# A recommender tower on one core: 24 steps in one table, another order of loads, and other shares for VectorE and GpSimd

## What is computed

```python
e = jnp.stack([tbl_0[ids[:, 0]], ..., tbl_31[ids[:, 31]]], axis=1)     # (512, 32, 16)
x0 = xk = e
for W in (W0, W1, W2):                                                # (32, hk, 64)
    xk = relu(einsum('bmd,bhd,mhk->bkd', x0, xk, W))
    outs.append(sum(xk, axis=2))
h = concatenate([concatenate(outs, axis=1), dense_ctx], axis=1)       # 192 + 16 columns
y = relu(relu(h @ W_top1 + b_top1) @ W_top2 + b_top2) @ W_top3
```

## Time and profile before

| | us |
|---|---|
| Median of 3 runs (380.64 to 382.44) | 381.08 |
| Span of the profiled execution, first to last instruction | 395.6 |
| TensorE matmuls busy | 292.4 (74%) |
| VectorE busy | 278.7 (70%) |
| GpSimd busy | 276.8 (70%) |
| ScalarE busy | 60.3 (15%) |
| Mean granted TensorE clock, 1.0 is full | 0.931 |
| Read from HBM | 60.17 MB |

### The profile page before, as it was taken

How to read it: one execution, slowest core, us unless ns; L and a number is a source line. 1 busy time by engine, 2 the same in 40 slices (tenths; PEclk the granted TensorE clock), 3 DMA queues, 4 the chain that set the end, 5 groups by cost and what they waited for, 6 DMA issues and landing times.

```text
span 395.6 us, 3778 instructions
## 1 busy us (share of the span) xinstructions
PE 292.4 (74%) x1252; PEld 94.2 (24%) x1252; DVE 278.7 (70%) x145; ACT 60.3 (15%) x72; POOL 276.8 (70%) x204
## 2 busy tenths in 40 slices
PE   0001400578979969998889599699849999999995
PEld 0000100222223313322223123132212333333341
DVE  0002200779978986999789779599799999999600
ACT  1001000221210312112120131121021022211021
POOL 5777772289999888999998885999980807856000
PEclk9999955699999996999999989699985999999999
DMA  7229589988522999978449899764289994340000
GB/s 220 43 52 300 161 292 337 335 262 252 170 63 85 270 338 324 311 232 319 110 116 276 303 325 344 243 218 96 49 288 317 332 285 146 99 106 13 2 13 0
DMA packets 35530, 79.59 MB, mean 201 GB/s; under 512 B 5984, under 2 KB 13536, under 8 KB 35520
## 3 DMA queue, kind: packets, MB, share of 16 engines
q1 hardware_dynamic: 22176, 61.63, 44.7%
q10 hardware_dynamic: 9248, 16.78, 15.8%
q0 software_dynamic: 4096, 1.06, 2.7%
HBM read 60.17 MB, written 2.10 MB: 157 GB/s over the span
## 4 chain that ended last, share of the span: by engine, by line
POOL 38%; PE 28%; issue 15%; another core or an unknown queue 9%; DMA 5%; ACT 2%; DVE 1%; ACTq 1%; SPq 0%; POOLq 0%; DVEq 0%
PE acc L626 25%; POOL pz L394 20%; POOL gathered L372 18%; DMA hidden<-relu_out 3%; PE spare L656 2%; DMA own<-fields 1%; ACT factor L497 1%; PE factor L650 1%; DMA gathered<-in_table,index 1%; ACTq L532 1%; DVE vz L446 1%; DMA stack<-feats 1%; PE acc L661 0%; DMA first_sb<-in_first_row 0%
## 5 line engine op out<-in xcount | busy, mean ns | idle before, releaser
L626 PE MATMUL acc<-vz,w_sb 128*64 128x512 f32 x896 | 216.0, 619 | 70.8 <-issue 37.9
L446 DVE TENSOR_TENSOR vz<-fields_sb,factor 128x2048 f32<-128x2048 f32 x93 | 206.9, 2280 | 17.4 <-PE acc L626 8.3
L394 POOL TENSOR_TENSOR pz<-fields_sb,hidden 128x1024 f32<-128x1024 f32 x64 | 151.8, 2381 | 47.0 <-DMA hidden<-relu_out 43.9
L372 POOL DMA_INDIRECT gathered<-in_table,index x128 | 123.0, 961 | 36.1 <-issue 34.9
L626 PEld LDWEIGHTS acc<-vz,w_sb 128*64 128x64 f32 x896 | 66.4, 143 | 207.5 <-issue 190.6
L626 PE MATMUL acc<-pz,w_sb 128*64 128x512 f32 x256 | 70.7, 631 | 22.2 <-POOL pz L394 22.1
L446 DVE TENSOR_TENSOR vz<-rotated,factor 128x2048 f32<-128x2048 f32 x16 | 36.1, 2283 | 64.0 <-issue 31.7
L497 ACT ACTIVATE factor<-hidden 128x1024 f32<-128x1024 f32 x31 | 31.5, 1026 | 101.6 <-DMA hidden<-relu_out 71.5
L522 ACT ACTIVATE relu_out<-acc 128x512 f32<-128x512 f32 x24 | 14.3, 596 | 153.4 <-PE acc L626 90.5
L626 PEld LDWEIGHTS acc<-pz,w_sb 128*64 128x64 f32 x256 | 16.9, 141 | 66.6 <-POOL pz L394 45.4
L442 DVE TENSOR_TENSOR vz<-opposite 128x256 f32<-128x256 f32 x8 | 15.8, 1980 | 8.0 <-PE acc L626 5.1
(11 more groups left out here) (13 smaller groups left out, 12.4 us busy)
## 6 DMA issues: line engine op xcount, KB each, us to landing
fields_sb<-fields SPq DMA_DIRECT2D x64, 512.0 KB, 7.0
rotated<-fields SPq DMA_DIRECT2D x32, 512.0 KB
hidden<-relu_out ACTq DMA_DIRECT2D x64, 256.0 KB
own<-fields SPq DMA_DIRECT2D x8, 512.0 KB
gathered<-in_table,index POOLq DMA_INDIRECT x128
fields<-gathered SPq DMA_DIRECT2D x16, 128.0 KB
opposite<-fields SPq DMA_DIRECT2D x8, 256.0 KB
w_sb<-in_w SPq DMA_DIRECT2D x2, 512.0 KB, 4.5
```

Of the source, the lines that this page charges most:

```text
L372: nc.gpsimd.indirect_dma_start(gathered[s][:, i, :], None, table, bass.IndirectOffsetOnAxis(ap=index[s][:, i:i + 1], axis=0)).then_inc(row ...
L394: nc.gpsimd.tensor_tensor(pz[:, slot, :], fields[s][:, t, :], hidden[s][:, g, :], ALU.mult).then_inc(pz_ready, 1)
L446: nc.vector.tensor_tensor(vz[:, slot, 0:nt, :], src[:, t:t + nt, :], factors[fslot][:, None, :].broadcast_to([P, nt, PAIR]), ALU.mult).the ...
L626: last = nc.tensor.matmul(acc[ab * HID:(ab + 1) * HID, bank, :], w_sb[layer][:, kt, :], z[:, ab * N:(ab + 1) * N], start=start, stop=stop)
```

## The change

The 24 steps stand in one table ORDER of (layer, pair) and are written out in full for all engines, with no loop on the chip. What changes:

- The order of the steps is another one; (1, 0) comes second, and the early part has two places where (2, x) stands two steps behind (1, x).
- GpSimd's tiles are given for each step (POOL_TILES, 2 to 5 of 16, all in the second half g = 1, 53 in all instead of 64); all eight tiles of g = 0 are VectorE's.
- VectorE multiplies up to four tiles in one instruction, into a `vz` ring of three slots of four tiles.
- The opposite product is made by GpSimd, into `oz`.
- Gathers: 32 before all else, then GATHERS_IN of them in each step, with four buffers for gathered rows; one addition makes all indices. In a layer-0 step the gathers stand ahead of the opposite product.
- `own`, `rotated` and `opposite` have one copy; SyncE's queue sends for each pair in turn: scratch, layer-0 operands, then all eight field tiles in order 0 to 7. The field tiles of pair p wait for the end of step (2, p - 2), the layer-0 operands for the product of (0, p - 1). Each pair has its own scratch area.
- Three factor buffers and three ReLU outputs instead of two (three in the prologue); VectorE's sums stand at least six tiles behind.

The core of the diff, the added functions with their lines of waits; what they replace is printed above:

```diff
-PROLOGUE = [(0, 0), (0, 1), (1, 0), (1, 1), (2, 0)]
-BODY = [(0, 0), (2, 1), (0, 1), (1, 0), (1, 1), (2, 0)]
...
+ORDER = [(0, 0), (1, 0), (0, 1), (2, 0), (1, 1), (0, 2), (2, 1), (0, 3),
+         (1, 2), (1, 3), (2, 2), (0, 4), (2, 3), (0, 5), (1, 4), (1, 5),
+         (2, 4), (0, 6), (2, 5), (0, 7), (1, 6), (1, 7), (2, 6), (2, 7)]
+STEPS = range(len(ORDER))
+POOL_TILES = {(1, 0): 2, (2, 0): 2, (1, 1): 2, (2, 1): 3, (1, 2): 3, (1, 3): 3, (2, 2): 3, (2, 3): 3,
+              (1, 4): 3, (1, 5): 3, (2, 4): 3, (2, 5): 4, (1, 6): 5, (1, 7): 5, (2, 6): 5, (2, 7): 4}
+FIRST_GATHERS = 2 * GATHERS
+GATHERS_IN = {(0, 1): 10, (2, 0): 6, (1, 1): 8, (2, 1): 10, (0, 3): 2, (1, 2): 9, (1, 3): 9,
+              (2, 2): 9, (2, 3): 9, (1, 4): 8, (1, 5): 8, (2, 4): 8}
+SPLIT = {8: (4, 4), 7: (4, 3), 6: (3, 3), 5: (3, 2), 4: (4,), 3: (3,), 2: (2,)}
+VTILES, VRING = 4, 3
+FRING = 3
+RRING = 3
+GRING = 4
...
+def vector_units(n):
+    layer, pair = ORDER[n]
+    if layer == 0:
+        return [(0, 0, 2), (0, 2, 2)] if pair == 0 else [(0, 0, L0TILES)]
+    if n == 1 or n == 3:
+        units = [(0, t, 2) for t in range(0, TILES, 2)]
+    else:
+        units = [(0, 0, 4), (0, 4, 4)]
+    t = 0
+    for nt in SPLIT[TILES - POOL_TILES[layer, pair]] if n < len(ORDER) - 1 else (2, 2):
+        units.append((1, t, nt))
+        t += nt
+    return units
+def pool_units(n):
+    layer, pair = ORDER[n]
+    if layer == 0:
+        return [(0, L0TILES)]
+    return [(1, t) for t in range(TILES - POOL_TILES[layer, pair], TILES)]
+def tensor_order(n):
+    v, p = len(vector_units(n)), len(pool_units(n))
+    if ORDER[n][0] == 0:
+        return [("v", u) for u in range(v)] + [("p", 0)]
+    order, done = [], 0
+    for u in range(v):
+        while done * v < (u + 1) * p and (n > 1 or u == v - 1):
+            order.append(("p", done))
+            done += 1
+        order.append(("v", u))
+    return order
...
-        own = [sb(f"own{s}", [P, PAIR]) for s in range(STREAMS)]
-        rotated = [sb(f"rotated{s}", [P, L0TILES, PAIR]) for s in range(STREAMS)]
-        opposite = [sb(f"opposite{s}", [P, 2, QCOLS]) for s in range(STREAMS)]
+        first_sb = sb("first_sb", [P, 1], I32)
+        index = sb("index", [P, PAIRS * GATHERS], I32)
+        gathered = sb("gathered", [P, GRING, GATHERS, DIM])
+        own = sb("own", [P, PAIR])
+        rotated = sb("rotated", [P, L0TILES, PAIR])
+        opposite = sb("opposite", [P, 2, QCOLS])
...
-        vz = sb("vz", [P, ZRING, 2, PAIR])
+        vz = sb("vz", [P, VRING, VTILES, PAIR])
...
+            def scratch(pair):
+                sp.wait_ge(rows_in[pair], 16 * GATHERS)
+                for c in range(2):
+                    copy = fields_dram[pair][c * FIELDS:(c + 1) * FIELDS, :]
+                    sp.dma_start(copy.rearrange("m (q x) -> (m q) x", q=QUART),
+                                 gathered[:, pair % GRING, :, :].rearrange("p b d -> p (b d)")) \
+                      .then_inc(scratch_in[pair % STREAMS][c], 16)
+            def layer0_operands(pair):
+                span = fields_dram[pair]
+                landed = 16 * (pair // STREAMS + 1)
+                sp.wait_ge(scratch_in[pair % STREAMS][0], landed)
+                if pair:
+                    before = step_of(0, pair - 1)
+                    sp.wait_ge(vz_ready, vectors_before(before + 1))
+                    sp.wait_ge(factor_ready, factors_before(before + 1))
+                sp.dma_start(own[:, :],
+                             span[0:FIELDS, None, :].broadcast_to([FIELDS, MREP, PAIR])).then_inc(own_in, 16)
+                sp.wait_ge(scratch_in[pair % STREAMS][1], landed)
+                sent = [own_in]
+                for t in range(L0TILES):
+                    turn = bass.AP(span.tensor, span.offset + MREP * t * PAIR,
+                                   [[PAIR, FIELDS], [PAIR, MREP], [1, PAIR]])
+                    if len(sent) >= IN_FLIGHT:
+                        sp.wait_ge(sent[-IN_FLIGHT], 16 * (pair + 1))
+                    sp.dma_start(rotated[:, t, :], turn).then_inc(rotated_in[t], 16)
+                    sent.append(rotated_in[t])
+                both = bass.AP(span.tensor, span.offset, [[QCOLS, P], [FIELDS // 2 * PAIR, 2], [1, QCOLS]])
+                sp.wait_ge(sent[-IN_FLIGHT], 16 * (pair + 1))
+                if pair:
+                    sp.wait_ge(pz_ready, pools_before(step_of(0, pair - 1) + 1))
+                sp.dma_start(opposite[:, :, :], both).then_inc(opposite_in, 16)
+            def field_tiles(pair, first, end):
+                span, s = fields_dram[pair], pair % STREAMS
+                landed = 16 * (pair // STREAMS + 1)
+                if pair >= STREAMS and first == 0:
+                    before = step_of(2, pair - STREAMS)
+                    sp.wait_ge(vz_ready, vectors_before(before + 1))
+                    sp.wait_ge(pz_ready, pools_before(before + 1))
+                for t in range(first, end):
+                    each = bass.AP(span.tensor, span.offset + MREP * t * PAIR,
+                                   [[0, HROWS], [PAIR, MREP], [1, PAIR]])
+                    if t >= IN_FLIGHT:
+                        sp.wait_ge(fields_in[s][t - IN_FLIGHT], landed)
+                    sp.dma_start(fields[s][:, t, :], each).then_inc(fields_in[s][t], 16)
+            scratch(0)
+            layer0_operands(0)
+            field_tiles(0, 0, TILES)
+            for pair in range(1, PAIRS):
+                scratch(pair)
+                layer0_operands(pair)
+                field_tiles(pair, 0, TILES)
...
+            def gather(i):
+                pair, b = divmod(i, GATHERS)
+                if b == 0 and pair >= GRING:
+                    for c in range(2):
+                        pool.wait_ge(scratch_in[pair % STREAMS][c], 16 * ((pair - GRING) // STREAMS + 1))
+                nc.gpsimd.indirect_dma_start(
+                    gathered[:, pair % GRING, b, :], None, table,
+                    bass.IndirectOffsetOnAxis(ap=index[:, i:i + 1], axis=0)).then_inc(rows_in[pair], 16)
+            def opposite_product(n):
+                pair = ORDER[n][1]
+                pool.wait_ge(opposite_in, 16 * (pair + 1))
+                if pair:
+                    pool.wait_ge(pz_used, pools_before(step_of(0, pair - 1) + 1))
+                nc.gpsimd.tensor_tensor(oz[:, :], opposite[:, 0, :], opposite[:, 1, :],
+                                        ALU.mult).then_inc(pz_ready, 1)
+            def product(n, u):
+                layer, pair = ORDER[n]
+                s = pair % STREAMS
+                g, t = pool_units(n)[u]
+                if layer == 1:
+                    pool.wait_ge(fields_in[s][t], 16 * (pair // STREAMS + 1))
+                if u == 0:
+                    pool.wait_ge(relayed[s][g], relay_count(n))
+                at = products_before(n) + u
+                if at >= PRING:
+                    pool.wait_ge(pz_used, PRODUCT_USED[at - PRING])
+                nc.gpsimd.tensor_tensor(pz[:, at % PRING, :], fields[s][:, t, :], hidden[s][:, g, :],
+                                        ALU.mult).then_inc(pz_ready, 1)
...
+            for i in range(FIRST_GATHERS):
+                gather(i)
+            sent = FIRST_GATHERS
+            for n in STEPS:
+                more = GATHERS_IN.get(ORDER[n], 0)
+                if ORDER[n][0] == 0:
+                    for i in range(sent, sent + more):
+                        gather(i)
+                    opposite_product(n)
+                else:
+                    units = len(pool_units(n))
+                    for u in range(units):
+                        product(n, u)
+                        for i in range(sent + more * u // units, sent + more * (u + 1) // units):
+                            gather(i)
+                sent += more
...
+                if u == 0 or vector_units(n)[u - 1][0] != g:
+                    dve.wait_ge(factor_ready, entry + 1)
+                for tile in range(t, t + nt):
+                    if layer == 0:
+                        dve.wait_ge(rotated_in[tile], 16 * (pair + 1))
+                    elif layer == 1 and g == 0:
+                        dve.wait_ge(fields_in[s][tile], 16 * (pair // STREAMS + 1))
+                if at >= VRING:
+                    dve.wait_ge(vz_used, at - VRING + 1)
+                src = fields[s] if layer else rotated
+                nc.vector.tensor_tensor(vz[:, at % VRING, 0:nt, :], src[:, t:t + nt, :],
+                                        factor[entry % FRING][:, None, :].broadcast_to([P, nt, PAIR]),
+                                        ALU.mult).then_inc(vz_ready, 1)
...
+            put_factors(0)
+            for n in STEPS:
+                after = n + 1 if n + 1 < len(ORDER) else None
+                if after is not None and source(after) < n:
+                    put_factors(after)
+                relu(n)
+                if ORDER[n][0] < 2:
+                    relay(n)
```

(35 more changed lines are left out.)

438 lines of the change are left out of this document (88 added, 350 removed).

## The result

The changed kernel takes 414.67 us (411.69 to 416.91, 4 runs), the kernel before beside it 381.59 (380.64 to 382.44, 4 runs): ratio 1.087, 95% interval 1.082 to 1.092. The forecast was 404.0 with 376 to 416: the side is right, the time 10.7 us short. The profiled execution took 416.91, its span 414.8. The experiments ran on other chips, where the kernel before takes 396 to 397 us and the changed one 414.56; there the ratio is 1.043 (1.039 to 1.048). In two experiments the profiled execution is a slow one, 4.6 and 7.2 us longer than any other of its kernel, which is said there.

A forecast was written before the change was run, and what follows sets the result against it. It took GpSimd to bound the kernel until 296 us, then TensorE, base 381.0. Walking the new order with its relay and operand waits gave 381.7, plus 2.0 for a low clock and 20.4 of tail: 404 us, range 376 to 416.

The forecast's parts named there:

- a chain in front and waits of the operands: Added cost: relay waits in early steps (VectorE idles 7.8 us), then layer-0 operands of pairs 3, 5, 7 late (22 for pair 3).
- the sum has 2.0: Term after pair 7's operand wait: TensorE's clock is low after an idle stretch, costing 2.0 us (0 to 4.3).
- The operands-in-time rival: Pair 3's scratch copy goes before 125 and nothing later waits, so VectorE bounds: 357 us; chance 0.17.
- The term that was too small: Layer-0 operands, scratch copy to last rotated tile in use: taken as 15 us, from rows of 14.4 to 17.5.
- The walk: Step-by-step sum of the changed kernel's times, from the first gathers at 43.7 us to 381.7, before clock and tail.
- The eight field tiles: Term on SP's queue: eight tiles take 4.6 + 4 x 1.75 = 11.6 us, bounds 9.2 and 13.8.
- The tail: Term for the end of the kernel, 395.6 - 375.2 = 20.4 us in the earlier profile, added unchanged.
- The step that took 4-tile products as a gain of 0.06 us each: VectorE's work: 235 tiles in 73 instead of 112 instructions, 0.064 us for each instruction, 270 us with sums.
- GpSimd as the bound of steps 8 to 12, 18.15 a step: Middle steps 8, 9, 10, 12: GpSimd's 3 products and 9 gathers take 18.15 us a step, over TensorE's 13.78.
- The step that took the wait of step 0 out of the profiled 395.6: Base: GpSimd's 14.61 us idle from a late first ReLU, taken as absent from timed runs, giving 381.0.
- The rival that rests on the Trainium skill: No fetch gaps: straight code saves one wait like the 4.0 us before a GpSimd gather, giving 400; chance 0.04.

## Why the prediction came out as it did

**The side is right, for its own reasons.** Less work and no contention, against a chain in front and waits of the operands: the opposite product is 0.74 us (predicted 0.73), VectorE's 4-tile product 4.34 from start to start (4.34), the GpSimd product with three gathers 6.00 and 6.05 (6.05). After pair 7's wait TensorE's first 16 matmuls took 5.85 us where later ones take 3.61, at a granted clock of 0.67 from 332 to 340: 2.2 us, for which the sum has 2.0. Step 1 starts at 55.70 (53.9), pair 3's scratch copy leaves at 149.92 (146.9), VectorE waits 18.47 (22), the last product of step 10 starts at 214.16 and ends at 216.52 (215.0). The operands-in-time rival asked for the scratch copy before 125; it left 25 us later, for the reason given against it: eight gathers behind a product that waits for a relay. The run that moves them confirms it with 17.5 us: this is the largest part of the loss.

**The term that was too small: 15 us from the scratch copy to the last rotated tile in use.** The walk used it for pairs 3, 5 and 7. It holds for pair 3, where nothing else is under way: 149.92 to 163.56, 13.6. For pair 5 it is 18.5 (227.82 to 246.31), for pair 7 20.6 (307.62 to 328.18), as the small copy, and with it the load that needs it, runs beside field tiles and a relay (which of the two costs how much isn't separated by a run): 6.0 and 7.5 us between them instead of 1.7. What was mis-sized is the choice of 15, near the row of an empty queue (14.4), for copies that the walk itself put right behind eight tiles. The other row (17.5) is of a copy behind four tiles, and there the first load follows in 4.3 us, at 135.38 behind 131.04:
```profile
135.38 0.53 SPq L287 DMA_DIRECT2D own<-fields  x1
```
Even 17.5 would have been too little for pairs 5 and 7.
Along the walk to the last ReLU (394.43, forecast 383.7) the 10.7 us are: 1.2 up to pair 5's scratch copy; 2.6 for its opposite product, done 19.8 behind it (17.2 in the walk); 1.1 in steps 14 to 16; -0.2 for the field tiles; 5.6 for pair 7's rotated tiles; 0.4 to the end. So 8.2 are this term. The tail is 20.4 as taken. The eight field tiles took 10.13 and 11.28, forecast 11.6. The walk adds up a span, and it was set equal to a time; a run's time is 1.8 to 2.1 us longer than its span (396.99 and 395.2, 416.91 and 414.8), so 2 us are missing in the sum. That it is off by 10.7 from the span and from the median (414.67) alike is chance: the profiled execution was 2.2 over the median.

**Costed too small: larger VectorE products.** The step that took 4-tile products as a gain of 0.06 us each left out that all behind them starts later; 2 tiles give 6.1 us back. The walk let VectorE finish a layer-0 product 4.34 behind the last rotated tile, where a split one finishes 2.29 behind it, three times on the path. That TensorE's earlier start in the other steps adds to it isn't shown.

**GpSimd as the bound of steps 8 to 12, 18.15 a step:** right as a pace (6.0 to 6.1 a product with three gathers), and near the edge: alone, a product less gave nothing, and GpSimd waited 13.5 us more for opposite operands; with the operands earlier it made the kernel slower, with VectorE busy for 94% of the stretch.

**The base.** The step that took the wait of step 0 out of the profiled 395.6 fitted the first chip's 381.08, though less well than within 0.1: a span of 381.0 is a time of 382.8. The other chips showed it to be part of the kernel before there: 396.9. The changed kernel has no gathers behind its first opposite product and takes 414.67 and 414.56 on both. So the loss is 33 us where the kernel before doesn't stand for it, and 18 where it does; the sign is the same. That on the first chip the timed runs have no late release is inferred, from 397 - 15.5 = 381.5 and from the changed kernel: its trace from that chip has the first ReLU 0.1 us behind the matmuls, all ten traces from other chips with 32 gathers in the first row have it 3.3 to 5.5 us behind. The first trace of the kernel before has the wait, but its span of 395.6 belongs to a run of some 397.4 us, not to one of the 380.6 to 382.4; the record doesn't say on which chip it was taken. What differs between the chips is open.

**Instruction fetch.** The rival that rests on the Trainium skill (Runtime: NRT & Kernel Launch, Instruction fetch mechanics) would have made the time 400. The waits of the changed kernel:
```profile
POOL gathered L318 <- issue: 33.2, 119, 0.3
```
The gaps ahead of gathers are 33.2 us in straight code, 34.9 in loops, and the one of 4.0 went, as that rule would have it. But in all three traces of the kernel before (4.0, 4.4, 4.1) it is the gap ahead of the 114th gather, seven products into the loop's second pass, and not at the jump. So a fetch isn't shown to be its cause, and no gain of its size can be told apart in a time that came out 10.7 above the forecast.

## What to carry to other kernels

An order written out by step moves waits rather than removing them: for each queue (an engine's and a DMA queue alike) ask what stands behind each instruction that waits, and put nothing there that a later stage needs before that wait ends. Price a small transfer at the place that it has in its queue, and with what other queues move at that time, not at its price when nothing else is under way. Split a product whose operands arrive one after the other. And when an engine is relieved without effect, look for the wait that takes the time up before deciding that it never was the bound.

## What the hardware showed unexpectedly

A long row of indirect DMAs on GpSimd can hold back the release of matmuls that are done: 25 us in the kernel before (matmuls done by 44.5, ReLU at 69.07); 18.5, 12.4 and 11.9 us in the run with more gathers early, and in all of these the ReLU followed the end of the row by 3 to 8 us. Shortening the row from 46 to 32 brought the ReLU from 68.78 to 48.98, which is still 5.5 us behind its matmuls. In nine traces of the changed kernel and its variants with 32 gathers in the first row, all from other chips than the first, it was 3.3 to 4.9 us late, in the one from the first chip 0.1. A row of eight behind an opposite product did it in one execution (ReLU at 126.75, matmuls done at 121.94; of 405.5 us, the longest of its eleven) and not in another (119.39, done at 119.34). The run with more gathers early was read in its longest execution too. What holds it back, how long a row has to be, and whether the recording of an execution takes part in it, wasn't settled.
